# Four-layer graph network on one Trainium2 core: layer 1's edge messages kept in two scaled fp16 parts and four buffers, edge features squared during edge placement, one one-hot buffer per slot chunk

## The reference

```python
edge_in = jnp.concatenate([edges, nodes[receivers], nodes[senders]], axis=-1)
h = jax.nn.relu(edge_in @ We1 + be1)              # one row of 128 per edge
new_edges = h @ We2 + be2
agg = jax.ops.segment_sum(new_edges, receivers, num_segments=nodes.shape[0])
h2 = jax.nn.relu(jnp.concatenate([agg, nodes], axis=-1) @ Wn1 + bn1)
new_nodes = h2 @ Wn2 + bn2
```

## Time and profile before

| | us |
|---|---|
| median of 3 runs | 4521.2 (4516.18 to 4568.18) |
| the profiled execution, as timed | 4529.34 |
| its span in the profile | 4527.7 |
| edge placement | about 110 to 555 |
| counts and layer 0 | 555 to 1896 |
| layer 1, edges: POOL's gathers | 1896.8 to 3209.9 |
| layer 1, edges: what is left after the last gather | to 3275 |
| layer 1's nodes, layers 2 and 3 | 3275 to the end |

### The profile page before, as it was taken

The page is one execution under the profiler, slowest core; times in us unless marked ns, Lnnn a source line. Parts: engine busy times, 40 slices in busy tenths (PEclk is TensorE's granted clock), DMA queues, the critical chain, the costliest instruction groups (busy, mean ns, idle before and its releaser), DMA issues. The chain is left out here.

```text
span 4527.7 us, 125847 instructions
## 1 busy us (share of the span) xinstructions
PE 3681.4 (81%) x48218; PEld 3245.1 (72%) x48218; DVE 2889.7 (64%) x3816; ACT 1598.7 (35%) x2668; POOL 2584.3 (57%) x2291
## 2 busy tenths in 40 slices
PE   0777699998899999499999999999766777777396
PEld 0565588887899999477777777777556667667396
DVE  6999888887111101588888888888546666666502
ACT  0333399998000000333333333333224444444200
POOL 0288877777666665187777777777203444444100
PEclk9767799999899999799999999999889999999698
DMA  5611188989999998488888888888507767777596
GB/s 162 245 30 30 43 293 323 331 326 329 332 400 378 418 417 340 159 272 273 260 265 265 263 262 267 266 267 268 205 24 249 265 222 248 251 235 245 170 404 248
DMA packets 430075, 1159.84 MB, mean 256 GB/s; under 512 B 111175, under 2 KB 250422, under 8 KB 422712
## 3 DMA queue, kind: packets, MB, share of 16 engines
q1 hardware_dynamic: 331478, 919.45, 57.1%
q0 software_dynamic: 66016, 114.12, 8.7%
q10 hardware_dynamic: 32256, 121.34, 6.9%
HBM read 791.79 MB, written 364.93 MB: 255 GB/s over the span
## 5 line engine op out<-in xcount | busy, mean ns | idle before, releaser
L930 POOL DMA_INDIRECT feat_slot<-SK,sidx_p x900 | 1116.7, 1241 | 407.5 <-issue 271.2
L972 POOL DMA_INDIRECT arena<-tab_l_src,SK x864 | 1006.3, 1165 | 397.7 <-issue 263.0
L854 POOL TENSOR_TENSOR arena<-arena 128x448 f16<-128x448 f32 x343 | 363.4, 1060 | 653.3 <-ACT arena L1729 653.1
L1270 PE MATMUL PS<-arena 128*128 128x192 bf16 (+1 forms) x7203 | 617.4, 248 | 105.8 <-DVE arena L2182 61.8
L1270 PEld LDWEIGHTS PS<-arena 128*128 128x128 bf16 x7203 | 607.8, 99 | 113.9 <-DVE arena L2182 62.1
L1437 PE MATMUL PS<-arena 128*128 128x128 f16 x4802 | 460.5, 223 | 134.6 <-DVE arena L2363 75.1
L1441 PE MATMUL PS<-arena 128*128 (+1 forms) x4802 | 439.6, 195 | 0.4 <-issue 0.4
L1437 PEld LDWEIGHTS PS<-arena 128*128 128x128 bf16 x4802 | 313.4, 99 | 161.7 <-issue 148.0
L1369 PE MATMUL PS<-arena 128*128 (+1 forms) x4178 | 416.8, 223 | 0.0
L1395 PE MATMUL PS<-arena 128*128 128x384 bf16 x2089 | 414.8, 336 | 2.1 <-DVE arena L2434 2.1
L2427 DVE TENSOR_TENSOR arena<-arena 128x896 f32<-128x896 f32 (+1 forms) x319 | 328.2, 1029 | 126.7 <-ACT arena L1769 118.6
(11 more groups left out here) (274 smaller groups left out, 6683.6 us busy)
## 6 DMA issues: line engine op xcount, KB each, us to landing
arena<-slot_rows SPq DMA_DIRECT2D x343, 448.0 KB
arena<-cnt_t SPq DMA_DIRECT2D x147, 896.0 KB
hots<-arena ACTq DMA_DIRECT2D x175, 672.0 KB
arena<-hots SPq DMA_DIRECT2D x175, 672.0 KB
arena<-cnt_t SPq DMA_DIRECT2D x147, 672.0 KB
cnt_t<-arena SPq DMA_DIRECT2D x49, 1568.0 KB
cnt_s<-arena SPq DMA_DIRECT2D x49, 1568.0 KB
arena<-cnt_s SPq DMA_DIRECT2D x49, 896.0 KB
```

Of the source, the lines that this page charges most:

```text
L854: pool.tensor_tensor(halves[i][:, n:2 * n], gated[i], halves[i][:, 0:n], ALU.subtract).then_inc(msg_lo, 1)
L930: pool.indirect_dma_start(feat_slot, bass.IndirectOffsetOnAxis(ap=sidx_p[odd][:, n:n + 1].bitcast(u32), axis=0), fwin[h][:, t * D:(t + 1) ...
L972: pool.indirect_dma_start(qgot[n % 3][:, slot_of[t] * P:(slot_of[t] + 1) * P], None, tab_src[4], bass.IndirectOffsetOnAxis(ap=gidx[odd][:, ...
L1270: last = nc.tensor.matmul(PS[:, at:at + w3], ring[u % RING][:, of:of + P], esplit[:, (i * CH + w) * w3:(i * CH + w + 1) * w3], start=u == ...
```

## The change

Layer 1's messages are kept as two fp16 parts, in buffers of their own for slot and natural units, two each. ACT's relu writes the first part as fp16; one DVE instruction takes the relu of the fp32 value again and subtracts the first part, writing the second as fp16. For a slot unit it reads the fp32 value from PSUM, for a natural one from `hid`, which now holds only the natural units' pre-activations. `last_part` is gone, PE sums two parts (256 columns), and PSUM is now free (`meet`'s wait) only after DVE's subtraction. With `agg_made` three and four units back the waits are looser:

```diff
-        hid = [carve(124 + 10.5 * i, 3 * CH * P) for i in range(2)]
+        hid = [carve(124 + 3 * i, TN * P) for i in range(2)]
+        halves_slots = [carve(130 + 3.5 * i, 2 * CH * P, f16) for i in range(2)]
+        halves_nat = [carve(137 + 3 * i, 2 * TN * P, f16) for i in range(2)]
...
+        def halves_of(j, odd, q):
+            kind, c = place(j, q)
+            return halves_slots[(c + odd) % 2] if kind == "slots" else halves_nat[c % 2]
...
                         if kind2 == "slots":
-                            pe.wait_ge(pre_free, slots_at(j2, c2))
+                            pe.wait_ge(msg_lo, count_at(j2, q2))
...
-                    parts = upper[(q + odd) % 2][:, 0:3 * n * H].rearrange("p (s b f) -> p s b f", s=3, b=n)
-                    o = PS[:, bank:bank + 3 * H].rearrange("p (s f) -> p s f", s=3)
+                    parts = halves_of(j, odd, q).rearrange("p (s b f) -> p s b f", s=2, b=n)
+                    o = PS[:, bank:bank + 2 * H].rearrange("p (s f) -> p s f", s=2)
...
-                        if not isinstance(j, int) or j > 0 or q >= 2:
-                            act.wait_ge(agg_made, count_at(j, q) - 2)
-                        nc.scalar.activation(hid[i][:, 0:CH * H], PS[:, i * 1024:i * 1024 + CH * H], ACT.Relu).then_inc(pre_free, 1)
+                        back = 2 if isinstance(j, int) and j == PAIRS_N else 3
+                        if not isinstance(j, int) or j > 0 or q >= back:
+                            act.wait_ge(agg_made, count_at(j, q) - back)
+                        nc.scalar.activation(halves_of(j, odd, q)[:, 0:CH * H], PS[:, i * 1024:i * 1024 + CH * H], ACT.Relu).then_inc(pre_free, 1)
                     else:
                         act.wait_ge(q_added, naturals_at(j, c))
-                        nc.scalar.activation(hid[i][:, 0:TN * H], hid[i][:, 0:TN * H], ACT.Relu).then_inc(relu_made, 1)
+                        if not isinstance(j, int) or j > 0 or q >= 4:
+                            act.wait_ge(agg_made, count_at(j, q) - 4)
+                        nc.scalar.activation(halves_of(j, odd, q)[:, 0:TN * H], hid[c % 2], ACT.Relu).then_inc(relu_made, 1)
...
-                    if not isinstance(j, int) or j > 0 or q >= 2:
-                        dve.wait_ge(agg_made, count_at(j, q) - 2)
...
-                    V.tensor_tensor(hid[i][:, n:2 * n], hid[i][:, 0:n], upper[i][:, 0:n], ALU.subtract).then_inc(msg_res, 1)
-
-                def last_part(j, odd, q):
-
-                    i = (q + odd) % 2
-                    n = (CH if place(j, q)[0] == "slots" else TN) * H
-                    dve.wait_ge(msg_res, count_at(j, q))
-                    V.tensor_tensor(hid[i][:, 2 * n:3 * n], hid[i][:, n:2 * n], upper[i][:, n:2 * n], ALU.subtract)\
+                    of = PS[:, i * 1024:i * 1024 + n] if kind == "slots" else hid[c % 2]
+                    to = halves_of(j, odd, q)
+                    V.scalar_tensor_tensor(to[:, n:2 * n], of, 0.0, to[:, 0:n], ALU.max, ALU.subtract)\
                         .then_inc(msg_lo, 1)
```

The slot one-hots get seven buffers, one per chunk, so that SP waits for the store of the same chunk a whole window ago; the feature buffers stay at four:

```diff
-        hotp = [carve(73.5 + 5.25 * i, HOTS, bf16) for i in range(4)]
+        hotp = [carve(kb, HOTS, bf16) for kb in (73.5, 78.75, 84, 89.25, 24.5, 29.75, 65.25)]
...
-                    if not isinstance(j, int) or j > 0 or c >= 4:
+                    if not isinstance(j, int) or j > 0:
                         sp.nop(nofuse=True)
-                        sp.wait_ge(hots_put[c % 4], j * (16 if c == 3 else 32) + 16 * (c // 4))
+                        sp.wait_ge(hots_put[c], j * 16)
```

```diff
+            def add_squares(n, odd, m):
+
+                act.wait_ge(fpiece_in[odd], m * 16 + (fpiece_from[odd] + 16))
+                nc.scalar.activation(fpiece[odd], fpiece[odd], ACT.Square, accum_out=fsum[:, bass.ds(n, 1)]).then_inc(fold_made, 1)
+                if isinstance(n, int) and n + 2 >= FPIECES:
+                    return
+                act.wait_ge(fold_made, n + 4)
+                of = feat.rearrange("(p n) f -> p (n f)", p=FPARTS)
+                act.dma_start(fpiece[odd], of[:, bass.ds((n + 2) * (FEDGES * D), FEDGES * D)]).then_inc(fpiece_in[odd], 16)
...
-                dve.wait_ge(total_made, 1)
+                scale_again()
```

More of the change, by code:

```diff
@@ L60 @@
 SEQ = 2 * NC - 1
+FPARTS, FPIECES = 125, 55
+FEDGES = E // FPARTS // FPIECES
 PLACES = PAIRS_N * SEQ + NC
@@ L1599, in keep_rows, with body @@
                         .then_inc(rows_kept, 1)
-                def body(w, odd, last=None):
+                def body(w, odd, last=None, squares=()):
                     if last is None or last < NB:
```

102 lines of the change are left out of this document (71 added, 31 removed).

## The result

| | before | after |
|---|---|---|
| median, us | 4543.3 (4 runs, 4516.18 to 4568.18) | 4486.77 (4 runs, 4473.85 to 4504.55) |
| ratio | | 0.9897, 95% interval 0.9851 to 0.9943 |
| profiled execution, as timed | 4529.34 | 4485.66 |
| its span | 4527.7 | 4484.0 |

The change makes the kernel 1.0% faster (1.2% by the two medians). The forecast said 3% (4387 us, range 4335 to 4485), and the measured median lies 2 us above the range. The forecast started from a median before of 4521.2 us; with a fourth execution (4565.39) that median is 4543.3.

A forecast was written before the change was run, and what follows sets the result against it. POOL's gathers were taken to bound layer 1's edges, held by DVE instructions with two SBUF inputs. Terms -117 (gathers), -22 (end) and +5 (squares) sum to -134 on a 4527.7 us span: 4387 us for the median, range 4335 to 4485.

The forecast's parts named there:

- Two fp16 parts: Layer 1's edges: one DVE pass less per unit shortens gathers from 1.165 to 1.03 us, 117 us less.
- can the others follow at 49.9?: Layer 1's edges: PE, DVE, DMA engines and ACT all stay under POOL's new period of 49.9 us per 13 units.
- Parts in four buffers: Layer 1's edges: relu and source addition no longer wait for the sum two units back; 0, hidden under POOL.
- Seven one-hot buffers: Layer 1's edges: 0 in the loop, behind POOL; 22 us less after the last gather, without waits for stored one-hots.
- where loads are there a unit takes 4.27: End of layer 1's edges: unit time with loads present, 4.27 us now and 3.9 with two parts.
- The bound that I named and did not take: End of layer 1's edges: gain 0 instead of 22 us if the four feature-load buffers take over.
- Squares: Edge placement: squares of the features on ACT cost 0 in the loop and 5 us at its end (3 to 12).
- a load of 960 KB (3.2 MB took 10.0, so 3 to 5.5): End of edge placement: each load of features to be squared takes 3 to 5.5 us.
- Rival D: Edge placement: late loads hold ACT, then DVE; at 25 us a load +181 us, in all 4568; chance 0.05.
- B: Layer 1's edges: gathers do not get shorter, only the end gains; 4504 us; chance 0.14.
- C: Layer 1's edges: DMA engines take over half way, 60 us goes instead of 117; 4444 us; chance 0.11.

The follow-up runs named there:

- e4_sbuf: Changed kernel with the second part of slot messages made from an SBUF tensor instead of PSUM: mean gather 1.094 us, first to last gather 1249.7 us.
- e9_four: Changed kernel with four one-hot buffers again instead of seven: first to last gather 1233.6 us, end 69.3 us.
- e8_two: Changed kernel with the waits for the sum two units back put in again: first to last gather 1195.5 us, ratio to before 0.9883.
- the repeat: Kernel before and changed kernel each profiled once more, unchanged: end 71.8 and 55.8 us, spans 4545.2 and 4460.6 us.
- e2_tail: Changed kernel with separate feature buffers for chunks 4 to 6 of the last window: end 47.3 us instead of 54.5.
- e5_small: Changed kernel with all piece loads but the first two cut to 4 KB, values summed instead of squares: placement loop 474.3 us, one-hots at 574.93.
- e7_all: Changed kernel with split piece loads, the last window's own feature buffers, later first loads and surplus squares moved to the start: median 4433.26 us, ratio to before 0.9792.
- e11_after: Changed kernel profiled once more, unchanged: span 4460.6 us, first to last gather 1198.7 us.

## Why the prediction was wrong

By its own steps:

1. *Two fp16 parts, -117.* The size came out right, in part by luck, and the attribution was not. A gather takes 1.035 to 1.039 us (forecast 1.03), the stretch 1202.3 and 1198.7 us (1196), 106 less than the mean of the two profiles of before. e4_sbuf shows the mechanism with its price. But "can the others follow at 49.9?" was answered from busy times of PE, DVE and DMA, and SP's queue was not among them. With two parts alone (e9_four) 13 units take 1233.6/24 = 51.4 us: 73 of the 106.
2. *Parts in four buffers, 0.* Right beside seven one-hot buffers (e8_two); beside four it was not tried.
3. *Seven one-hot buffers.* That they are worth 0 in the loop held only while POOL was slow; under shorter gathers they are worth 33 us (e9_four). That this did not show in the total is luck: what step 1 claimed too much, step 3 claimed too little. At the end -22 was -9 in the recorded pair, -16 in the repeat. The step that failed is "where loads are there a unit takes 4.27": loads were not there. The bound that I named and did not take, that the four feature buffers take over, is what happened. Own buffers give 7 us (e2_tail), not the whole rest.
4. *Squares, +5.* It was +53 and +52: this is the term that carries the miss. The square (1.80 us) and the new scale (4.2) were right, and so was the 0 for the loop as far as ACT's time goes (e5_small). Wrong was "a load of 960 KB (3.2 MB took 10.0, so 3 to 5.5)". I scaled by bytes from a transfer over 128 partitions to one over 125, which runs five packets at a time. Those pieces come one in 8.7 us. The closing squares at that pace are the wait of 35 us at the end. In the loop, beside other traffic, they come one in 9 to 10 us for most of it, more than the 8.8 us of a window, which makes the 20. Two pieces ahead of the last window loads are the 5 at the start, which I had at 0 (with those two issued later, e7_all starts at 79.89). Rival D had the mechanism: a late load holds ACT, and that holds DVE. It asked when one load takes longer than two windows (17.6 us), not how often a piece can arrive when both in flight share the same few engines, and it priced the loop alone, not the end.
5. *What lies around.* The forecast was a difference applied to a profile of 4527.7 us with the node products at full clock. The changed kernel was first profiled with them at half: 22 us of the 90 between forecast sum and measured difference. Each kernel was seen at both levels; whether the change moves the odds is open, so these 22 us are neither for nor against it.

So, from -134 to -43.7: +48 placement, +13 end, +22 clock, +6 gathers, +1 counts. Rivals B and C are excluded by the gathers' mean and by the stretch of 1202 us. The sign and the mechanism of the main term held. The median missed the range by 2 us only, and with the split load alone it is 4446, well inside. At the other clock the changed kernel would be inside too (e11_after, 4462), but the load is where the reasoning failed: +53 against a band of 3 to 12.

## What to carry over

Do not scale a transfer's time by its bytes across shapes: look up a row with the same number of partitions, or at what the program does elsewhere (here `dst`, also 125 partitions, is loaded as 112 + 13, and the 127 of x as 112 + 15). When a bound engine gets faster, list what it hid until now, queues of waits included (SP waited 311 us for stores under POOL), and treat edits that seem worth nothing as possible carriers of the gain. An edit that repeats one stage's work at its close must be costed at the close, bare, with its loads at their own pace.

## What the runs showed of the hardware

- A load of 937.5 KB over 125 partitions takes 8.7 us a piece with two in flight, and its queue has five packets running at one time, hardly ever more; while the slot table is cleared from another queue, all traffic together is 240 GB/s beside such loads and 384 beside loads of 112 + 13 partitions. I had expected 3 to 5.5 us. A clearing of 40 MB that ended at 181.8 us before ended at 465.4 beside such loads.
- `scalar_tensor_tensor` with one input in PSUM and one in SBUF, fp32 with fp16, holds no indirect transfer's descriptor generation (0.946 us for 110 that began in it); with both in SBUF the same instruction of 1.088 us holds it to its end (1.83 us for the one shown, 1.353 on the mean of 96).
- PE, fully busy behind a pause of 19.3 us, ran 196 fp32 matmuls at a granted clock of 0.50 in nine of thirteen profiled executions (50 us) and at 0.99 to 1.00 in four (26 us), with both kernels on both sides. It moves the total by up to 22 us, half a per cent, where this change brings 1.0 to 1.5.
